# Layer 1 of a graph and expert network: another way from its attention to its experts

## The reference

```python
x = x + gnn(layernorm(x))
x = x + moe0(layernorm(x))                # heads, experts of width 1024, shared expert of 2048
x = x + relu(res + agg)                   # 12 heads over the edges, softmax for each target node
xn = rms_norm(layernorm(x), norm_w)
probs = softmax(xn @ router_w.T)          # 8 experts
sel   = one_hot(top_k(probs, 2))
h = silu(xn @ gate_w.T) * (xn @ up_w.T) * (probs * sel)   # expert width 1536
x = x + layernorm(x) + h @ down_w.T
```

## Time and profile before

| | us |
|---|---|
| median of 3 runs | 1762.14 |
| the profiled execution | 1764.23 |
| its span, first to last instruction | 1762.7 |
| PE busy | 1477.7 (84%) |
| DVE busy | 1275.7 (72%) |
| ACT busy | 867.7 (49%) |
| POOL busy | 301.5 (17%) |

### The profile page before, as it was taken

One profiled execution on the slowest core, in us unless ns is written; L12 is line 12 of the kernel. 1 busy time (PEld: TensorE's weight loads), 2 busy tenths in 40 slices (PEclk: granted clock), 3 DMA queues, 4 the chain that ended last, 5 costly groups with the idle time before them and its releaser, 6 DMA issues. The chain is left out here.

```text
span 1762.7 us, 36531 instructions
## 1 busy us (share of the span) xinstructions
PE 1477.7 (84%) x14413; PEld 1259.6 (71%) x14413; DVE 1275.7 (72%) x2159; ACT 867.7 (49%) x1215; POOL 301.5 (17%) x252
## 2 busy tenths in 40 slices
PE   7987868886989999999993689830799999999990
PEld 5664446664667899999991544420799999999990
DVE  8996377774656688888874589461688888888872
ACT  1112037776334577777761145520666666666650
POOL 0003006661130000000002067604100000000003
PEclk9998889998999999999995779855899999999995
DMA  7620000004465788898863001004988888888854
GB/s 201 152 66 0 1 9 1 1 1 135 143 209 180 246 299 298 295 306 299 297 210 101 12 29 35 16 0 116 318 299 294 292 291 303 296 292 299 297 200 143
DMA packets 57168, 307.57 MB, mean 174 GB/s; under 512 B 14539, under 2 KB 14789, under 8 KB 33292
## 3 DMA queue, kind: packets, MB, share of 16 engines
q1 hardware_dynamic: 42380, 269.61, 45.1%
q0 software_dynamic: 14720, 37.05, 7.8%
HBM read 273.16 MB, written 33.42 MB: 174 GB/s over the span
## 5 line engine op out<-in xcount | busy, mean ns | idle before, releaser
L582 PE MATMUL ps<-big,wh 128*128 128x176 f16 x2184 | 502.3, 240 | 8.6 <-DVE wl L511 5.6
L586 PE MATMUL ps<-big,wl 128*128 128x176 f16 x2184 | 502.5, 238 | 0.0
L584 PE MATMUL ps<-big,wh 128*128 128x176 f16 x2184 | 502.4, 238 | 0.0
L603 PE MATMUL ps<-big,wh 128*128 128x176 f16 x2160 | 262.8, 238 | 0.0
L603 PE MATMUL ps<-big,wl 128*128 128x176 f16 x1080 | 248.9, 239 | 0.0
L511 DVE SCALAR_TENSOR_TENSOR wl<-raw,wh 128x2304 f16<-128x2304 f32 x94 | 239.7, 2550 | 1.5 <-ACT wh L455 1.5
L511 DVE SCALAR_TENSOR_TENSOR wl<-ext,wh 128x2304 f16<-128x2304 f32 x90 | 229.7, 2552 | 0.6 <-issue 0.5
L455 ACT ACTIVATE wh<-raw 128x2304 f16<-128x2304 f32 x94 | 198.9, 2117 | 60.0 <-PE ps L603 58.3
L582 PEld LDWEIGHTS ps<-big,wh 128*128 128x128 f16 x2184 | 211.4, 97 | 9.6 <-DVE wl L511 6.0
L455 ACT ACTIVATE wh<-ext 128x2304 f16<-128x2304 f32 x92 | 194.7, 2117 | 43.3 <-PE ps L603 42.1
L584 PEld LDWEIGHTS ps<-big,wh 128*128 128x128 f16 x2184 | 213.9, 98 | 0.1
(11 more groups left out here) (300 smaller groups left out, 2677.5 us busy)
## 6 DMA issues: line engine op xcount, KB each, us to landing
raw<-in_units SPq DMA_DIRECT2D x56, 1152.0 KB, 5.5
ext<-in_units SPq DMA_DIRECT2D x55, 1152.0 KB, 5.8
raw<-in_units SPq DMA_DIRECT2D x38, 1153.0 KB
ext<-in_units SPq DMA_DIRECT2D x37, 1153.0 KB, 6.4
raw<-in_units_s SPq DMA_DIRECT2D x16, 769.0 KB
ext<-in_units_s SPq DMA_DIRECT2D x16, 769.0 KB, 4.3
big<-x_slots POOLq DMA_DIRECT2D x20, 528.0 KB, 8.7
y_slots<-big POOLq DMA_DIRECT2D x20, 528.0 KB, 5.1
```

The costliest lines, as they stand in the source:

```text
L582: nc.tensor.matmul(o, wh[:, u % RING, w_], x_, start=c == 0 and m == 0, stop=False, skip_group_check=True)
L584: nc.tensor.matmul(o, wh[:, u % RING, w_], xTl[:, c, 0:ph.n], start=False, stop=False, skip_group_check=True)
L586: ins = nc.tensor.matmul(o, wl[:, u % RING, w_], x_, start=False, stop=c == KC - 1, skip_group_check=True)
L603: ins = nc.tensor.matmul(o, l_[:, u % RING, w_], r_, start=first and k == 0 and c % 2 == 0, stop=last and k == 2, skip_group_check=True)
```

## The change

In layer 1, from the last head to the first expert:

- **Statistics between heads.** relu(z) is added to `xres` and `bn_stats` taken by quarters of the columns (`mixed(q)`, one STT instruction over 5 x 192 columns and five `bn_stats`): quarters 0 and 1 on DVE after the shifts of heads 8 and 11 (at h = 5 and h = 8), quarter 2 at h = 11, quarter 3 after the last head. The root mean square of the second norm is worked out from the variance of the first (two columns `pair`), so the squares and their root fall away.
- **Rows without the weight vector.** `row_scaled` writes `z` with both norms and without `norm_w`; the weight is folded into the router's matrix `g16` (`wcol`, between the layers) and applied when rows enter a pass. POOL makes `xf = z * vec` for the scatter (5 instructions), and before that `rowl = z - rowh` (5), where `rowh` is ACT's float16 copy.
- **Logits by tile**: 12 matmuls of 16 columns for each tile, written as rows, so that `logits_back` and the copy before it fall away (in layer 0 too). **Choice on logits** (`logits_joined`, `chosen`): fewer DVE steps, and the exponent (`chances_asked`, `shares`) comes after the slots.
- **First pass's rows by matrix products**: DVE makes one-hot matrices `place` (`placed`, ten instructions of 125 x 176), PE multiplies `rowh` and `rowl` with them (60 matmuls), ACT and DVE split. The fences F_GAT and F_ROUTE1 are gone; `scatter(1)` runs beside this.
- **Weights early**: SP loads the first three units of expert 0 as soon as the heads are done, and goes on once the table is there.
- **The join** `xres + z` of layer 1 runs on POOL in pass 0 (`row_joined(t)`: a subtract-and-multiply that makes layernorm's z again, then an add), tile t once unit 2t is through `up`. In layer 0 DVE does the join, at j = 8 to 12.
- In both layers the first pass stores nothing, the number of passes is read earlier in layer 0 (at j = 18), and there PE's wait for `s_shv` before the loop is gone. POOL makes two more constants at the start.

```diff
+            def row_joined(t):
+                pool.wait_ge(ph_1.up, 2 * t + 1)
+                nc.gpsimd.tensor_scalar(z[:, t, :], xres[:, t, :], mv[:, t, 0:1], pair[:, 3, t, 0:1],
+                                        ALU.subtract, ALU.mult).then_inc(s_joined, 1)
+                pool.wait_ge(s_joined, NT + 2 * t + 1)
+                nc.gpsimd.tensor_tensor(xres[:, t, :], xres[:, t, :], z[:, t, :], ALU.add).then_inc(s_joined, 1)
...
-            rows_in(0)
+            if ph is ph_0:
+                rows_in(0)
+            pool.wait_ge(ph.xt, 3)
+            rows_in(1)
             meanwhile()
-            with pool.Fori(0, n_pass) as i:
+            pool.wait_ge(ph.yr, 4)
+            pool.sem_inc(ph.yfree, 1)
+            with pool.Fori(1, n_pass) as i:
...
-            fence(pool, F_GAT)
+            for t in range(NT):
+                pool.wait_ge(s_split, t + 1)
+                nc.gpsimd.tensor_tensor(rowl[t], z[:, t, :], rowh[:, t, :], ALU.subtract).then_inc(s_rest, 1)
+            pool.wait_ge(s_vec[1], 32)
+            for t in range(NT):
+                nc.gpsimd.tensor_tensor(xf[:, t, :], z[:, t, :], vec[:, 1, :], ALU.mult).then_inc(s_xf, 1)
+            pool.wait_ge(s_xf, NT)
             scatter(1)
-            fence(pool, F_ROUTE1)
-            ffn_pool(pool, ph_1, passes(pool), lambda: join(1))
+            pool.wait_ge(s_tab, 2)
+            ffn_pool(pool, ph_1, passes(pool), rows_joined)
...
+            def mixed(q):
+                own = slice(q * D // 4, (q + 1) * D // 4)
+                dve.wait_ge(s_gadd, 3 * q + 3)
+                step(nc.vector.scalar_tensor_tensor(out=xres[:, :, own], in0=z[:, :, own], scalar=0.0,
+                                                    in1=xres[:, :, own], op0=ALU.max, op1=ALU.add))
+                for t in range(NT):
+                    ins = nc.vector.bn_stats(st[:, t, q, :], xres[:, t, own])
+                return ins
...
+                if h in (5, 8, 11):
+                    mixed((h - 5) // 3)
             sums_inverted(H - 1)
-            dve.wait_ge(s_gadd, H)
...
-            layernorm()
-            rmsnorm(1e-6, 1, 32)
...
             slots()
+            placed()
+            chances_asked()
+            low, x_low, hidden = e1 = vector_steps(dve, ph_1)
+            low(0, 0)
             table()
-            fence(dve, F_GAT)
-            fence(dve, F_ROUTE1)
...
+            for k in range(3):
+                for c in range(2):
+                    at = (2 * k + c) * 128
+                    for t in range(NT):
+                        for part in (rowh[:, t, :], rowl[t]):
+                            ins = nc.tensor.matmul(x_bank(k, ph_1)[:, c, :], part[:, at:at + 128], place[:, t, :],
+                                                   start=t == 0 and part is not rowl[t],
+                                                   stop=t == NT - 1 and part is rowl[t])
+                ins.then_inc(ph_1.xt, 1)
```

More of the change, by code:

```diff
@@ L784, in _ @@
             pool.wait_ge(s_tab, 1)
[L785 removed]
+            ffn_pool(pool, ph_0, passes(pool), lambda: None)
             fence(pool, F_EXP0)
@@ L1152, in transposed_out, with gates_split @@
                     count["tp"] += 1
+            def gates_split(layer):
+                step(nc.vector.tensor_scalar(g16[:, layer, :, 0:NE], gates[:, layer, :, :], WS, None, ALU.mult))
+                step(nc.vector.scalar_tensor_tensor(out=g16[:, layer, :, NE:2 * NE], in0=gates[:, layer, :, :],
+                                                    scalar=WS, in1=g16[:, layer, :, 0:NE], op0=ALU.mult,
+                                                    op1=ALU.subtract))
             def row_stats(t):
@@ new lines, in shares @@
+            def shares(layer):
+                dve.wait_ge(s_sel, layer + 1)
+                step(nc.vector.tensor_reduce(best, e9[:, :, 0:NE], AX.X, ALU.add))
+                step(nc.vector.reciprocal(wts[:, 0, :], best))
+                step(nc.vector.tensor_tensor(wts[:, 1, :], e9[:, :, NE], wts[:, 0, :], ALU.mult))
+                if layer == 0:
+                    step(nc.vector.tensor_scalar(wts[:, :, :], wts[:, :, :], 1e-7, None, ALU.max))
+                    step(nc.vector.memset(cmb[:, :, :], 1.0))
+                    step(nc.vector.tensor_tensor(eq, oh[:, 0], bc(wts[:, 0, :]), ALU.mult))
+                    step(nc.vector.tensor_tensor(lg2, oh[:, 1], bc(wts[:, 1, :]), ALU.mult))
+                    nc.vector.tensor_tensor(cmb[:, :, 0:NE], eq, lg2, ALU.add).then_inc(s_cm, 1)
@@ L1441, in passes_counted @@
             def passes_counted(layer):
                 dve.wait_ge(s_rk, layer + 1)
-                step(nc.vector.tensor_copy(s8[:, 0, :], counts))
-                step(nc.vector.tensor_scalar(s8[:, 1, :], s8[:, 0, :], float(B), None, ALU.is_gt))
-                for k in range(2, (T - 1) // B + 1):
-                    step(nc.vector.scalar_tensor_tensor(out=s8[:, 1, :], in0=s8[:, 0, :], scalar=float(k * B),
-                                                        in1=s8[:, 1, :], op0=ALU.is_gt, op1=ALU.add))
@@ L1450, in passes_counted @@
-                at = 1
-                for k, d in enumerate((1, 2, 4)):
-                    step(nc.vector.tensor_copy(s8[:, 2 + k, :], s8[:, at, :]))
-                    step(nc.vector.tensor_tensor(s8[:, 2 + k, d:NE], s8[:, at, d:NE], s8[:, at, 0:NE - d], ALU.add))
-                    at = 2 + k
-                step(nc.vector.tensor_tensor(s8[:, 5, :], s8[:, at, :], s8[:, 1, :], ALU.subtract))
+                step(nc.vector.tensor_tensor(more, counts.unsqueeze(2).to_broadcast([P, NE, 3]), over[:, :, :],
+                                             ALU.is_gt))
@@ L1567, in _ @@
                     table()
+                if j == 8:
+                    chances_asked()
+                if j == 10:
+                    shares(0)
+                if j == NS + 2:
+                    dve.wait_ge(s_tab, 1)
+                    n_pass = passes(dve)
                 if j + 1 < 2 * NS:
@@ L1952, in _ @@
             for t in range(NT):
-                rows_turned(0, t)
+                rows_turned(0, xf, t)
             shared_first(0)
-            logits(0)
+            for t in range(NT):
+                logits(0, t)
             for j in range(2 * NS):
```

365 lines of the change are left out of this document (208 added, 157 removed).

## The result

The changed kernel took 1714.71 us (median of 4 runs, 1706.86 to 1724.05) against 1762.45 for the kernel before; the ratio is 0.9734 (95% interval 0.9678 to 0.9789). The profiled execution took 1706.86 us, its span 1705.3. Executions of this kernel lie further apart than those of the kernel before (ten over 22 us; twelve of the kernel before over 17), for a reason that the experiments found outside the places that the prediction looked at, so the two are compared by stretches of the trace first.

The account below looks back on a forecast made before the run. PE bounds the passes; the gap between heads and layer 1's passes is one chain. 56 + 9.7 - 11 - 1 - 5 - 0.3 = 48.4 us off the profiled 1764.23: 1715.8, or 1714 on the median's scale; range 1698 to 1731.

Parts of the forecast that it names:

- After G: Layer 1, from the last head's add into z to `up(0, 0)`: 41 us against 98.3, so 57.3 less.
- the port in the choice: Layer 1's choice: DVE instructions reading SBUF alone stop while POOL multiplies; 4.5 us, bounds 0 and 8.8.
- Join in pass 0: Layer 1, pass 0: DVE's SBUF instructions wait for POOL's `row_joined` and PE loses time; 11 us lost, range 3 to 20.
- Ramp 1.3 and rows 1: Layer 1, pass 0: units 1 and 2 about 1.3 us late; pass 1's rows, scatter beside weights, 1 lost, bounds 0 and 8.
- Heads: In the heads, `mixed(0)` and `mixed(1)`, 2.45 us each, lie in DVE's line: 5 lost, bounds 3 and 7.
- Layer 0: Layer 0: join off POOL 6.2, logits 1, pause before the passes 2.5; together 9.7 us saved.
- Start: Start of the program: two more constants delay DVE, 0.3 us lost.
- Rival (a): POOL is cheap: single-instruction port waits, short subtract-and-multiply; join 4, choice 1.5, 1704 us; chance 0.27.
- (b): Pass 0 starves, PE stopping behind `low` or at pass 1's rows: join 20, rows 4, choice 8, 1729 us; chance 0.24.
- (c): Later passes pay for late rows and weights, 3 us in each of 8 passes: 1738 us; chance 0.02.
- (d): Slower: the scatter gets no turn behind the weight stream, PE waits at unit 7 for pass 1's rows: 1777 us; chance 0.03.
- the three signs that I had said would prove me wrong: PE's idle in pass 0 under 3 or over 20 us, slots after +38, or heads over 7 more.

Follow-up runs that it names:

- the repeat: The changed kernel run again, unchanged: 1709.21 us median, 1706.36 to 1728.64.
- the second trace: Trace of the changed kernel when run again, unchanged; its traced execution took 1706.5 us.
- the experiment: Changed kernel with the three earlier quarters of relu and statistics moved after the last head: lowest 1709.84 us, median 1716.33.
- the first trace of before: Profiled execution of the kernel before, 1764.23 us; the second is from running that kernel again, unchanged: 1760.62 us median of twelve runs.
- two traces of edited ones: Changed kernel with layer 0's join back on POOL, 1715.44 us median; the same with its adds begun with DVE's copy, 168.6 us first transposes to first `up`.

## Why the prediction was right, and where it was not

The forecast was 1714 and the four runs' median 1714.7; ten runs with the repeat have 1711.3. The agreement is partly luck. The sum was made against the profiled execution and gave 48.4 less; the profiled one after was 57.4 less, and the median lies nearer only because other executions have longer heads. Of the 9 us between, the join, the heads and layer 0 came out some 15 better than the sum, the ramp with the rows and the start some 5 to 6 worse. Term by term:

- **After G, 57.3 expected, 57.7 measured.** Row 0 +5.4 (5.6), logits +19.9 (18.6; a logit pair took 0.117), slots +32.2 (30.7), products +34.7 (33.5, 7.0 long for 6.1: half clock until 1175), `up(0, 0)` +41 (40.6). The term that was only a guess between 0 and 8.8, the port in the choice, was right at 4.5 (4.0). The Trainium skill (SBUF — State Buffer, section "SBUF: two separate sides") gives the shared pair to whoever starts first for one whole instruction: the trace agrees for the products (three waits, each within one product of 1.77), though it gave three waits where I had made one of it, and two reductions between them waited for nothing; the copies of 8.99 and 6.05 us go beyond it.
- **Join in pass 0, 11 expected, 3.5 measured** (1.8 in the second trace, 1 to 2 by leaving it out). The step that failed is "of the three SBUF instructions of a unit each waits for one of POOL": `low` never waits, it makes POOL wait; and the subtract-and-multiply, 2.93 long (2.66 by L756's rate), holds DVE 0.7 only. Length was read as hold. The estimate of 0.7 us from the Trainium skill (GPSIMD Engine Reference, section 3.1), meant for the instruction's length, is what DVE loses and not the 2.93 of the row; the loss of 6 that I made of it was still too high. The upper case of the term was also summed wrongly: 2.7 units of 5.8 less 1.7 are 14, not 16.
- **Ramp 1.3 and rows 1 expected, some 6 measured.** The three first units lost 7.6 where those of the kernel before had lost about 2, and the rows nothing; in the second trace it is 5.8 and 2.5. The rows said 15 us of transfers for the scatter at a share of 0.85 and I put it at the wrong place: the scatter does not meet pass 1's rows first but unit 3's weights, which wait for the table (ACT idles 8.6 us for them; they landed some 12.5 us after their issue, where the median of such a block is 6). ACT began on them at +53.7; for `up(0, 3)` at its pace (+52.0) it should have been +47.3, since ACT's and DVE's halves take 2.1 and 2.6. The second cause, DVE's register read between `hidden(0, 0)` and `low(0, 2)`, was not in the sum at all.
- **Heads, 5 expected, 1.2 measured** in the first pair of traces (1.7 by the experiment). I had taken POOL's waits for DVE as proof that DVE never waits; before the last head it waits some 18.7 us for ACT and PE.
- **Layer 0, 9.7 expected; 13.2 measured against the first trace of before and 8.6 against the second.** The join's 6.2 was the size of one execution; in the second the whole stretch is only 2 to 4 longer than after, and on POOL it needn't cost anything. The way into the passes gave 4.9 instead of 2.5: the pause of 3.06 (0.28 after) and the low clock behind it (0.61 from 603 to 607) are most of it; the rest wasn't split.
- **Start, 0.3 expected, 1.9 measured**, which says nothing: over the 14 traces the first transpose of layer 0 lies anywhere from 417.1 to 422.7.
- Rival (a) was nearer than the forecast on the join, the forecast on the choice. (b) named the right meeting, scatter against the tightest time; its victim, the rows of pass 1, was hit in the second trace and not in the first. (c) and (d) did not come: the later passes keep 51.6 us. The scatter took 41 us where I had 34 and the kernel before 29; the Trainium skill (DMA: Bandwidth & Descriptors, section "Queues, rings and completion order") has the queues take turns, and the trace agrees, with each slowed and none stopped.

Of the three signs that I had said would prove me wrong, PE's idle time in pass 0 was about 9 us (the units lost 11 in all, low clock included), well within 3 to 20; but only 2 of the 9 stood beside the join. A sign that sums two causes can't tell them apart.

## What to carry to other kernels

When a gap is closed, list everything that it had been giving time to, and place each on the new clock: here a scatter, a weight fetch behind a table, a register read and a join all came to stand beside the first units. Where two waits end within a microsecond or two, mending one can show nothing; try both together before dropping either. Read a cost that a profile shows once from a second execution before it goes into a sum, and compare stretches rather than whole times when some stretch varies by itself.

## What the runs showed of the hardware that I had not expected

- POOL's tensor-and-scalar instruction over 768 columns lasts 2.93 us and costs DVE 0.7; its add lasts 1.77 alone and 2.31 beside `low`, where it waits for DVE and then holds it (1.51 us for an instruction of 0.26).
- Beside POOL's products two DVE reductions of one SBUF tile took their 0.20 us, while three DVE instructions with two SBUF inputs, of 0.20 us each alone, took 1.47 to 1.72.
- Five POOL adds in a row kept a DVE copy waiting to their end in two traces of one kernel (8.99 and 6.05 us), and let DVE in after each add in two traces of edited ones (0.54, 2.03, 3.36 us). Open, as told above.
- In the heads PE can meet the level of 1.2 GHz in some executions and not in others, with the same code of the heads: heads of 10.0 us become 13.6, and the twelve heads 147.0 instead of 128.8.
- A single DVE register read with the entry into the loop behind it left DVE idle for 1.05 us in one kernel and 2.0 in another; the read itself took 0.86 and 1.82 us, beside transfers at a share near 1.
